# Two attention and two feed-forward layers on one core: second attention on a window of 36 columns, weights laid out by the host, every engine's list in a new order

## What is computed

```python
def _L0_xcond_ref(query, key, value, tau, delta, Wq, bq, Wk, bk, Wv, bv, Wo, bo):   # H = 16, DK = 16
    q = _split_heads(query @ Wq.T + bq)
    k = _split_heads(key @ Wk.T + bk)
    v = _split_heads(value @ Wv.T + bv)
    scores = jnp.einsum('bhqd,bhkd->bhqk', q, k)
    scores = scores * tau[:, :, None, None] + delta[:, None, None, :]
    scores = scores / jnp.sqrt(jnp.asarray(DK, scores.dtype))
    p_attn = jax.nn.softmax(scores, axis=-1)
    x = jnp.einsum('bhqk,bhkd->bhqd', p_attn, v)
    x = x.transpose(0, 2, 1, 3).reshape(query.shape[0], -1, H * DK)
    return x @ Wo.T + bo
...
def _L0_ffn_ref(x, w1, conv_w, conv_b, w2):   # act_quant per row, weight_quant per matrix
    h = bit_linear(x, w1)
    h = depthwise_conv1d(h.transpose(0, 2, 1), conv_w, conv_b)
    h = h.transpose(0, 2, 1)
    h = jax.nn.silu(h)
    return bit_linear(h, w2)
...
def _L1_xcond_ref(encoder_outputs, decoder_h_t, src_len, p_t, W_a, W_c):   # WINDOW = 16, DEV_POW = 128
    attn_start = jnp.maximum(p_t - WINDOW, 0.0)
    attn_end = jnp.minimum(p_t + WINDOW, src_end)
    mask = (idx[None, :] < attn_start[:, None]) | (idx[None, :] > attn_end[:, None])
    score = jnp.einsum('nqh,hk,nlk->nql', decoder_h_t, W_a, encoder_outputs)
    score = jnp.where(mask[:, None, :], -1000000000.0, score)
    align = jax.nn.softmax(score, axis=2)
    gauss = jnp.exp(-(idx[None, :] - p_t[:, None]) ** 2 / DEV_POW)
    align = align * gauss[:, None, :]
    context = jnp.einsum('nql,nlh->nqh', align, encoder_outputs)
    cat = jnp.concatenate([context, decoder_h_t], axis=2)
    return jnp.tanh(cat @ W_c.T)
...
def _L1_ffn_ref(x, W1, b1, W2, b2, Wr, br):   # E = 8 experts, one per row, gated
...
x = x + _L0_xcond_ref(_layernorm(x), ctx_1024, ctx_1024, condB_tau[:, None], fside_BxS2_0, ...)
x = x + _L0_ffn_ref(_layernorm(x), ...)
x = x + _L1_xcond_ref(ctx_1024, _layernorm(x), _lenS2, condB_pt, L1_xcond_W_a, L1_xcond_W_c)
x = x + _L1_ffn_ref(_layernorm(x), ...)
```

## Time and profile before

| | us |
|---|---|
| median of 3 runs | 556.01 (555.12 to 561.21) |
| the profiled execution | 554.58 |
| its span, first to last instruction | 552.8 |
| TensorE busy | 384.9 (70%) |
| VectorE busy | 305.0 (55%) |
| ScalarE busy | 188.4 (34%) |
| GpSimd busy | 116.1 (21%) |

### The profile page before, as it was taken

The page is one execution under the profiler, slowest core; times in us unless marked ns, Lnnn a source line. Parts: engine busy times, 40 slices in busy tenths (PEclk is TensorE's granted clock), DMA queues, the critical chain, the costliest instruction groups (busy, mean ns, idle before and its releaser), DMA issues. The chain is left out here.

```text
span 552.8 us, 8359 instructions
## 1 busy us (share of the span) xinstructions
PE 384.9 (70%) x2897; PEld 301.2 (54%) x2897; DVE 305.0 (55%) x810; ACT 188.4 (34%) x464; POOL 116.1 (21%) x130
## 2 busy tenths in 40 slices
PE   4434725839977887988898877881556108999995
PEld 3223524628655565665575654660444107988993
DVE  2793510693895793995995965953631511322330
ACT  2025113344454453454464451450401003223330
POOL 1954201301301301311320220010000350212221
PEclk9987957865979978979979887696755657999999
DMA  7435956545546645255262261119954141101110
GB/s 229 108 99 106 222 125 123 183 123 107 192 116 117 206 125 108 66 127 118 76 140 74 80 116 54 39 46 321 332 142 164 33 141 70 49 28 56 51 33 12
DMA packets 53084, 64.35 MB, mean 116 GB/s; under 512 B 12933, under 2 KB 45736, under 8 KB 53040
## 3 DMA queue, kind: packets, MB, share of 16 engines
q1 hardware_dynamic: 37916, 43.79, 32.5%
q10 hardware_dynamic: 13956, 17.23, 9.6%
q0 software_dynamic: 1168, 2.76, 1.6%
HBM read 49.35 MB, written 14.94 MB: 116 GB/s over the span
## 5 line engine op out<-in xcount | busy, mean ns | idle before, releaser
L569 PE MATMUL ps<-W 125*32 125x112 f32 (+2 forms) x1280 | 99.9, 283 | 33.1 <-DMA W<-d_nm 13.5
L569 PEld LDWEIGHTS ps<-W 125*32 125x32 f32 (+2 forms) x1280 | 69.5, 136 | 57.8 <-issue 19.9
L573 PE MATMUL ps<-idf,hold 125*128 125x125 f32 (+4 forms) x200 | 39.0, 308 | 64.5 <-DVE hold L1472 22.7
L1580 DVE TENSOR_REDUCE mx<-ps 112x1 f32<-112x375 f32 x128 | 61.5, 540 | 26.5 <-PE ps L569 26.2
L998 ACT ACTIVATE hold<-ps 128x224 f32<-128x224 f32 (+4 forms) x80 | 33.2, 430 | 115.6 <-PE ps L573 69.8
L573 PEld LDWEIGHTS ps<-idf,hold 125*128 125x128 f32 (+4 forms) x200 | 27.1, 167 | 73.0 <-DVE hold L1472 25.7
L569 PE MATMUL ps<-hold 128*128 128x128 f32 (+2 forms) x320 | 61.2, 358 | 1.6 <-ACT hold L998 1.0
L569 PE MATMUL ps<-hold,proj 128*128 128x128 f32 (+2 forms) x288 | 52.0, 333 | 4.4 <-ACT hold L998 3.9
L569 PEld LDWEIGHTS ps<-hold 128*128 128x128 f32 (+2 forms) x320 | 50.4, 239 | 7.7 <-ACT hold L998 2.8
L1147 ACT ACTIVATE W<-ps 125x448 f32<-125x448 f32 x96 | 44.8, 545 | 25.6 <-PE ps L569 25.4
L569 PEld LDWEIGHTS ps<-hold,proj 128*128 128x128 f32 x288 | 40.2, 198 | 15.2 <-ACT hold L998 6.3
(11 more groups left out here) (151 smaller groups left out, 516.9 us busy)
## 6 DMA issues: line engine op xcount, KB each, us to landing
W<-in_L_ffn_W ACTq DMA_DIRECT2D x16, 1024.0 KB, 9.3
hold<-in_ctx SPq DMA_DIRECT2D x16, 375.0 KB
d_k<-W SPq DMA_DIRECT2D x8, 562.5 KB, 4.4
W<-d_k SPq DMA_DIRECT2D x8, 562.5 KB
hold<-d_mask SPq DMA_DIRECT2D x8, 492.2 KB, 3.8
d_xs<-hold SPq DMA_DIRECT2D x1, 3598.0 KB, 21.1
hold<-d_xs SPq DMA_DIRECT2D x12, 257.0 KB, 2.7
W<-d_k SPq DMA_DIRECT2D x8, 375.0 KB
```

What stands on the lines that cost most here:

```text
L569: return pe.matmul(o, lhsT=l, rhs=r, start=start, stop=stop, skip_group_check=True)
L573: return pe.transpose(o, i, ident[0:n, 0:n])
L1580: dve.tensor_reduce(mx[:, h:h + 1], pS[h % 3][0:T, 0:L], X, ALU.max).then_inc(mx_done, 1)
```

## The change

- Host: ctxT (context transposed), WqT, WkT, WvT, WoT, WcT, WaT, w1T and w2T come already transposed, and one array consts holds all small tables and the identity. w_tr, w_sb, the context load cx and its transposes are gone. w_quant has two steps per matrix on VectorE, and ScalarE's w_cast writes the bf16 weights.
- Second attention: per batch a window of WN = 36 columns starting at s0 (read by the engine from s0i). p_ew copies those columns of cxT to ew; p_cm (GpSimd) and p_cu (ScalarE) sum the context columns weighted by ge into a 37th, for batches whose window is empty. p_G multiplies ew by WaT and p_V2 multiplies it by WcT ahead of time; so u_sc is on 36 columns, u_alT is one transpose, u_c is gone, and u_wc is one product with V2 and two with xn2T.
- x3 and its normalisation stay in xall in SBUF; d_x3, d_xn3, d_mask and d_nm are gone, and the nm rows go from nmT to qst in three SBUF to SBUF transfers.
- Normalisations 0, 2 and 3 are applied on ScalarE with a bias nmr = -mean * rstd from GpSimd; normalisation 1 stays on VectorE. The query bias moves to ScalarE. The left tap of the convolution is two multiplications and two additions on GpSimd (t_tap, t_conv).
- a_scores makes two heads in the two banks of pS, and one reduction takes both maxima; the transposed scores have two banks pE of their own.
- Zeroing of d_xs: seven transfers of 256 rows on ScalarE's queue, one per turn. Experts 0 to 2 are loaded in one place of ScalarE's list (w_early), experts 3 to 7 by SyncE.
- Every engine's loop list is in another order, with batches up to eight turns apart.

```diff
@@ block.sync @@
+            @batch
+            def p_kread(b):
+                sp.wait_ge(k_written, 16 * (b + 1))
+                if b == 0:
+                    sp.wait_ge(delta_written, 16)
                 if b >= 2:
                     sp.wait_ge(st_ps, 12 * (b - 1))
...
             def a_stack(b):
                 sp.wait_ge(nmT_sb, b + 1)
-                sp.dma_start(d_nm[b % 2], nmT[:, :]).then_inc(nm_written, 16)
-                sp.wait_ge(nm_written, 16 * (b + 1))
-                sp.dma_start(qst[b % 2][KD:KX].rearrange("p h t -> p (h t)"), d_nm[b % 2].rearrange("(t h) n -> t (h n)", t=3)).then_inc(nm_loaded, 16)
+                if b >= 2:
+                    sp.wait_ge(st_ps, 12 * (b - 1))
+                for t in range(3):
+                    sp.dma_start(qst[b % 2][KD + t:KD + t + 1], nmT[16 * t:16 * t + 16, :]).then_inc(nm_loaded[b % 2], 16)
...
+            sp.wait_ge(pv_ps, NG * B)
+            for e in range(3, NE - 1):
+                load_expert(sp, e)
             sp.wait_ge(x2_ready, B)
+            sp.wait_ge(cm_made, B)
+            load_expert(sp, NE - 1)
@@ block.tensor @@
+            def p_G(b):
+                for m in range(DC):
+                    for k in range(DC):
+                        last = mm(pY[:, WC * m:WC * m + WC], WaT[:, k, 128 * m:128 * m + 128], ew[b % 2][:, k, :], k == 0, k == DC - 1)
+            def p_V2(b):
+                for k in range(DC):
+                    last = mm(pY[0:WC, 0:D], ew[b % 2][:, k, :], WcT[:, k, :], k == 0, k == DC - 1)
-            def a_scores(b, h):
+            def a_scores(b, i):
+                if b >= 1 or i >= 1:
+                    pe.wait_ge(mx_done, NP * b + i)
+                for n in range(2):
+                    last = mm(pS[0:T, n, 0:L], qst[b % 2][0:KD, 2 * i + n, :], kst[b % 2][0:KD, 2 * i + n, :], True, True)
@@ block.scalar @@
+            def w_early(b):
+                if b == 0:
+                    act.wait_ge(quant, 2)
...
+                    for e in range(3):
+                        load_expert(act, e)
+            def w_zero(b):
+                if b < NB * 128 // ZR:
+                    act.dma_start(d_xs[ZR * b:ZR * b + ZR, :], A["zeros"]).then_inc(zeroed, 16)
+            def p_cu(b):
+                for k in range(DC):
+                    last = act.activation(prod[:, k, :], prod[:, k, :], ACT.Copy, accum_out=ew[b % 2][:, k, WN:WC])
@@ block.gpsimd @@
+            def p_cm(b):
+                pool.tensor_tensor(prod, cxT[b % 2], ge.unsqueeze(1).to_broadcast([128, DC, L]), ALU.mult).then_inc(cm_made, 1)
+            def t_tap(b, half):
+                pool.tensor_tensor(th[:, ms, :], hs[:, ms, 0:T], cw[:, ms, 0:1].to_broadcast([128, M0 // 2, T]), ALU.mult)
+            def t_conv(b, half):
+                pool.tensor_tensor(yc[:, ms, :], yc[:, ms, :], th[:, ms, :], ALU.add).then_inc(yl_done, 1)
+            def ln_rstd(which, b):
+                step(pool.tensor_tensor(rstd[:, which, s], ve[:, which:which + 1], expo[0:T, :], ALU.pow))
+                pool.tensor_scalar(nmr[:, which, s], mv[:, which, 0:1], rstd[:, which, s], -1.0, ALU.mult, ALU.mult)
@@ block.vector @@
+            def p_ew(b):
+                s0 = dve.value_load(s0i[0:1, b:b + 1], min_val=0, max_val=L - WN)
+                dve.tensor_copy(ew[b % 2][:, :, 0:WN], cxT[b % 2][:, :, bass.ds(s0, WN)]).then_inc(ew_made, 1)
+            def a_max(b, i):
+                dve.wait_ge(s_ps, NP * b + i + 1)
+                dve.tensor_reduce(mx[:, 2 * i:2 * i + 2], pS[0:T, :, 0:L], X, ALU.max).then_inc(mx_done, 1)
-            for i in range(-1, B + 3):
-                t_x2(i - 3)
+            for i in range(B + 8):
+                w_small(i)
+                u_sc(i - 6)
```

1555 lines of the change are left out of this document (775 added, 780 removed).

## The result

The changed kernel takes 514.93 us (median of 4 runs, 514.46 to 515.26), the kernel before in the same job 555.57 (4 runs): 0.9285 of it, 95% interval 0.9246 to 0.9324. It is faster, by 7% and not by the 17% forecast, and 515 lies above the range of 424 to 498. Some executions of a kernel are 1.5% or more longer than its shortest, at a lower granted clock: the ratios leave them out, and the traces of c0, e1, e5 and f6 are of such executions.

What follows compares the result with a forecast made beforehand. It took a ring through SyncE to bound the kernel, 32.0 us a full gap. Start 51.8, seven gaps 227, drain 42, second attention and router 16.6, routing and experts 119.3 make 456.7 of span: forecast 460 us, range 424 to 498.

Steps and rivals of the forecast that it cites:

- The engines' sums: Busy time in a full gap between nmT copies: TensorE 28.1 us, VectorE 25.2, ScalarE 20.6, GpSimd 15.4.
- rival 1: VectorE and GpSimd hinder each other partly in the gaps: 5 us more a gap, 495 us; chance 0.20.
- the ring: Through SyncE: nmT, nm issues, context, x, kst reload, next batch's scores and maxima; 31.9 us, taken as 32.0 a full gap.
- the rule that the prediction weighed: VectorE and GpSimd share ports held for a whole instruction, so right taps, silu and hq would wait.
- phase of maxima: First score to last maximum of a batch: VectorE's 16.5 us of work plus 1.0 handing over, 17.5.
- the start: Before the first nmT: first key product 11.5 us, first scores 36.4, first phase 15.4, nmT at 51.8.
- The third gap: w_early's six 1 MB expert loads block ScalarE some 8 us and share with the reload: 10 more, 42 us.
- The drain: Last nmT to last x2: 53.8 us less 3, 8.7 and 1, plus 1 for GpSimd's convolution: 42.
- 2 (no ring): The ring does not bind; VectorE's 25.2 us is the floor: gap 27.5, 428 us; chance 0.17.
- 4: Complete port contention: GpSimd's 15.4 us in series inside the ring, 47.3 us a gap, 567 us; chance 0.03.
- 3: At the ends ScalarE stays blocked by loads, 13 us, and the drain keeps 10 more: 483 us; chance 0.07.
- a gap above 40: Sign in the gaps between nmT copies that would make the prediction wrong by more than its range.

Runs made afterwards that it cites:

- c0: The changed kernel run again unedited, as control: 511.8 us, 0.910 of the kernel before.
- e1: Changed kernel without reading the keys of batches 2 to 7 back into kst (wrong scores, only prices the reload): 476.7 us.
- e5: Changed kernel with w_early issuing one expert's two loads in each of three turns instead of six loads in one: 512.6 us, 0.911.
- f6: f2 without the reload of kst from batch 2 on (wrong scores, only prices it): 472.1 us, 0.857.
- e2: Changed kernel with SyncE issuing the reload of kst in front of the loads of context and x: 516.6 us, 0.943.
- e4: Changed kernel with 32 matmuls that nobody reads in front of a batch's first scores, in TensorE's wait for the reload: 507.6 us, 0.926.
- f5: f2 with the score banks handed over one head at a time instead of in pairs: 467.6 us, 0.854.
- f2: f1 with SyncE issuing x, then the reload of kst, then the context, in place of context, x, reload: 481.4 us, 0.871.
- e3: Changed kernel with ready TensorE work moved in front of a batch's first scores to fill the wait for the reload, one VectorE step moved: 508.6 us, 0.928.
- f4: f2 with the last batch's turn reordered on TensorE, ScalarE and VectorE: its own work first, older batches' second attention and routers behind: 491.9 us, 0.886.
- f1: Changed kernel with the edits of e12 (late expert loads) and e3 (work filling the wait) together: 489.7 us, 0.879.
- f3: f2 with 12 matmuls that nobody reads in front of the first scores of a batch: 487.6 us, 0.876.
- e12: Changed kernel with w_early's six expert loads moved behind the last pv, to SyncE's four others: 499.0 us, 0.903.

## Why the prediction was wrong

**The engines' sums** held, to 0.7 us each but for GpSimd (18.5 for 15.4): three nmr took 3.8 us and three rstd 3.0 in the fifth gap, where undisturbed ones take 0.27 and 0.58. That is rival 1 in small, and mostly on the other side: GpSimd waits more than VectorE. VectorE waits too. Its scaling of a diagonal in t_q2 takes 0.27 us undisturbed, in the kernel before always (0.27 to 0.28), and in the fifth gap it ended with GpSimd's subtraction over 750 columns:

```profile
243.26 0.76 DVE L1518 TENSOR_SCALAR W<-consts,tiny 112x112 f32<-112x112 f32 x1
```

```profile
242.38 1.57 POOL L1354 TENSOR_TENSOR W<-W 128x750 bf16<-128x750 f32 x1 [0.40 <-ACT W L982]
```

It stands in front of the last maximum, so the 0.3 to 0.5 us that it loses in a full gap are in the ring (1.35 and 0.9 in the second and third gap, 0.8 to 1.05 in the full gaps of e1). Four right taps, 1.06 us elsewhere, took 1.83 in the seventh gap. e1, which leaves all of GpSimd's work and has gaps of 29.8, shows that the port does not hold the gap at 36. By the rule that the prediction weighed (the Trainium skill, SBUF — State Buffer, "Who interferes with whom") the two share ports, and the trace agrees with it for nmr beside VectorE's right taps and silu, and for this scaling beside the subtraction.

**The ring** was named rightly (e1: 6.2 us of a full gap) and summed too short. Its four terms in the fifth gap, the longest of the full ones, against the prediction's:

| term | forecast | after | from |
|---|---|---|---|
| last maximum to nmT | 2.1 | 1.75 | 244.87 to 246.62 |
| issues in front of the reload | 1.7 | 3.2 | 209.22 to 212.42 |
| reload | 10.6 | 12.1 | 212.42 to 224.54 |
| phase of maxima | 17.5 | 20.3 | 224.54 to 244.87 |
| sum | 31.9 | 37.4 | |

Over the fourth to seventh gap the means are 1.75, 2.8, 11.3 and 19.8, 35.6 in all, so the phase is the largest part of the miss. The issues were a mis-sized term: three nm issues take 1.78 us and context and x 0.9 with the steps between. The reload too: in e2, where the context stood behind it, it took 10.9 for 12.1. The phase is the step that failed: I summed VectorE's work in it, added 1.0 for handing over and put the clock at nothing. After a wait of up to 6 us TensorE had its work there at half clock, and was busy 19.8 of the 20.4 us, VectorE 14.8. The prediction said itself, of the earlier trace rows, that an idle stretch costs more than its length, and then left that out of the sum; e4 prices it at 1.8 us a gap, and with the clock kept up the phase is 17.6 to 17.9 us, close to the 17.5 of the sum. That the number fits then is in part luck, for it was summed as VectorE's, and in e4 TensorE is the fuller engine, 17.1 of 18.0 us for VectorE's 15.6. The statement that the eight double maxima cost 6.8 to 7.6 was right (7.5), but their price is not their duration: two heads in one wait make the engines take turns. Single banks gave 3.6 to 3.9 us in the first phase in three pairs of kernels, and in the gaps 1.9 in a full one but 4.3 over all seven (f5 against f2, where the clocks differ too). That also bears on the start, 3.9 us over: the first key product (11.40 for 11.5) was right, the first scores came at 38.06 for 36.4, and the rest is the first phase, 17.6 for 15.4; with single banks (f5) it is 13.1.

**The third gap**, 50.9 for 42, was the right mechanism, 9 us too small: ScalarE was blocked 19.76 us where I scaled 13.71 us for eight loads down to 8 for six. The eight met a DMA share of 0.11 in the 5 us before them; these six met the d_k write, nm rows, context, x and the reload. And the block was not the cost: e5 removes it and gains nothing.

**The drain** (58.4 for 42) failed in a step, not in a size. ScalarE's block did go (no issue wait behind the last pv), as did u_c from the front. But I took them off 53.8 us as if the rest stood where it was. The new lists carry each batch longer: from nmT(b) to x2(b) it takes 73.0 to 75.0 us in batches three to five (the first is zero), in place of 51.4 to 54.2. So at the last nmT more of batch six is undone; its x2 before and after:

```profile
366.51 0.48 DVE L1712 SCALAR_TENSOR_TENSOR hold<-ps,tiny,hold 112x256 f32<-112x256 f32 x1 [0.75 <-PE ps L569]
```

```profile
350.95 0.48 DVE L1766 SCALAR_TENSOR_TENSOR hold<-ps,tiny,hold 112x256 f32<-112x256 f32 x1
...
375.05 0.48 DVE L1766 SCALAR_TENSOR_TENSOR hold<-ps,tiny,hold 112x256 f32<-112x256 f32 x1
```

That is 13.3 us behind the last nmT before (353.23) and 34.3 after (316.62), and the last x2 follows it by 40.7 us before and 24.1 after. The last pv, with batch six's work between, came 24.7 us behind nmT in place of 17.0, at a mean clock of 0.57, for 0.80 before. The second thing left out is that clock: f6 against f2 prices it at 6.5 us of the drain with the same lists, though not in the changed kernel's order, where 55.0 and 58.4 were seen. So an order can be credited only where the clocks of the two traces agree, and neither e3's nor f4's does. What decides whether the clock is back at 1.00 15 us behind nmT (e3, f1, f2, f3, f5) or stands at 0.50 up to 27 (the changed kernel, f6) stays open.

**Right to within 1.5 us:** second attention and router at the end (17.3 for 16.6), routing and experts, and that the expert loads stay hidden under them, even with 6 MB more (e12). **Rivals:** 2 (no ring) is what e1 shows, as a kernel and not as the changed one; its gap of 27.5 was 29.8. 1 (port, 37 us a gap) has nearly the measured number but not the cause: VectorE lost 0.3 to 0.5 us by it in a full gap. 4 did not come. 3 named the right place, the drain, for another reason. The sentence that a gap above 40 would break the range came true in one gap only, for which the prediction itself had 42; five gaps of 34.6 to 37.4 and the drain did as much.

## What to carry to other kernels

When a wait is the bound, list what each engine has deferred behind it, and price the stretch after the wait for the engine that idled, at the clock the idling left it, and not only for the engine that is busiest on average. Moving that work into the wait pays only if the hand-over between the engines does not become the bound behind it (e3). Before an order of the lists is credited with a gain, compare the granted clock of the two traces stretch by stretch (f2 and f6). Order on a shared in-order DMA list by who waits: small rows that release an engine first, then the bulk that ends the ring, then loads that are early anyway, and never in it a load that itself waits for a buffer. When all lists are re-ordered, compare how long one item stays in the pipeline (here nmT to x2, 51 to 54 us before and 73 to 75 after) before subtracting anything from the drain.
